# A two-layer kernel on one Trainium2 core: the skewed read of the attention band and the buffers around it

## The reference

```python
x = L0_attn_x                                   # (4, 512, 128) f32
xn = _layernorm(x)
x = x + _L0_attn_ref(xn, ...) + _L0_ffn_ref(xn, ...)      # windowed attention; 16 experts, top 4
xn = _layernorm(x)
return x + _L1_attn_ref(xn, ...) + _L1_ffn_ref(xn, ...)   # full attention; 8 experts, top 2
```

```python
strain = disp_win - disp[:, :, :, None, :]                # (B, nh, T, 64, 16)
logits = gelu(strain @ W_strain + rel_emb @ W_pos) @ W_bond - 10.0 * sigmoid(gelu(strain @ W_dmg + b_dmg) @ W_dmg_out + b)
weights = softmax(where(cmask, logits, -inf), axis=-1)    # over the 64 positions
out = einsum('bntd,bntde->bnte', weights, val_win) @ W_cproj
```

## Time and profile before

| what | value |
|---|---|
| median of 3 runs | 1331.48 us (1328.04 to 1336.38) |
| the profiled execution | 1326.2 us |
| its span | 1324.5 us |
| mean granted TensorE clock | 0.889 of full speed |
| busy | PE 80%, DVE 74%, ACT 62%, POOL 10% |
| first band stage | about 339.6 to 432.3 us of the span |
| second band stage | about 719.0 to 818.3 us |

### The profile page before, as it was taken

How to read it: one execution, slowest core, us unless ns; L and a number is a source line. 1 busy time by engine, 2 the same in 40 slices (tenths; PEclk the granted TensorE clock), 3 DMA queues, 4 the chain that set the end, 5 groups by cost and what they waited for, 6 DMA issues and landing times. The chain is left out here.

```text
span 1324.5 us, 22974 instructions
## 1 busy us (share of the span) xinstructions
PE 1055.4 (80%) x9629; PEld 545.8 (41%) x9629; DVE 981.5 (74%) x1266; ACT 816.5 (62%) x857; POOL 127.7 (10%) x218
## 2 busy tenths in 40 slices
PE   2589999989578599999997468765669989998787
PEld 1233333333466133333333458332235646555332
DVE  6799999999533999999996425349648566666746
ACT  1689999999442699999996512310155564665354
POOL 3000000000100000000001001405400000000630
PEclk9799999999788799999999678775679898999788
DMA  7300000000392200000000860002113432422110
GB/s 259 102 2 1 1 2 1 2 2 1 87 246 52 49 1 1 1 1 2 1 1 0 229 154 21 0 0 82 46 30 99 128 96 81 143 75 62 46 35 24
DMA packets 66886, 71.71 MB, mean 54 GB/s; under 512 B 5892, under 2 KB 58592, under 8 KB 65760
## 3 DMA queue, kind: packets, MB, share of 16 engines
q1 hardware_dynamic: 63456, 49.28, 12.7%
q0 software_dynamic: 3328, 20.98, 6.9%
HBM read 46.12 MB, written 20.97 MB: 51 GB/s over the span
## 5 line engine op out<-in xcount | busy, mean ns | idle before, releaser
L535 DVE SCALAR_TENSOR_TENSOR ring<-AD,PT 128x1808 f32<-128x1808 f32 (+15 forms) x128 | 284.3, 2221 | 3.8 <-POOLq L517 3.2
L680 PE MATMUL LG<-ring,lred 128*32 128x456 f32 (+15 forms) x2048 | 232.2, 573 | 1.3 <-ACT ring L632 1.3
L1598 ACT ACTIVATE EX<-SS 128x1024 f32<-128x1024 f32 x128 | 130.9, 1028 | 105.3 <-PE SS L1469 104.4
L1687 DVE TENSOR_REDUCE MX<-SS 128x2 f32<-128x1024 f32 x128 | 153.0, 1215 | 52.8 <-PE SS L1469 52.3
L622 ACT ACTIVATE ring<-ring 128x3616 f32<-128x3616 f32 (+15 forms) x50 | 169.9, 3399 | 3.7 <-DVE ring L535 3.7
L702 PE MATMUL SD<-DS,eyes 96*32 96x456 bf16 (+15 forms) x2496 | 157.5, 372 | 9.2 <-ACT ring L627 7.2
L630 ACT ACTIVATE ring<-ring 128x1824 f32<-128x1824 f32 (+15 forms) x78 | 141.0, 1808 | 0.0
L702 PEld LDWEIGHTS SD<-DS,eyes 96*32 96x32 bf16 x2496 | 58.1, 96 | 152.9 <-ACT ring L627 57.3
L1469 PE MATMUL SS<-KS,QS 32*128 32x512 f32 x256 | 75.2, 585 | 51.1 <-DVE MX L1687 46.0
L535 DVE SCALAR_TENSOR_TENSOR ring<-AD,bdmg 128x1808 f32<-128x1808 f32 (+15 forms) x50 | 110.7, 2214 | 0.0
L715 PE MATMUL PY<-w2T,xg 128*128 128x128 f32 x512 | 74.2, 288 | 35.2 <-DVE xg L560 35.2
(11 more groups left out here) (300 smaller groups left out, 1486.7 us busy)
## 6 DMA issues: line engine op xcount, KB each, us to landing
wide<-band POOLq DMA_DIRECT2D x16, 1024.0 KB, 11.5
w1s<-in_L_ffn_W SPq DMA_DIRECT2D x39, 256.0 KB, 3.0
w2s<-in_L_ffn_W SPq DMA_DIRECT2D x39, 256.0 KB, 3.0
band<-zs SPq DMA_DIRECT2D x8, 1024.0 KB, 8.3
band<-Z SPq DMA_DIRECT2D x4, 1024.0 KB, 8.7
xs<-Z SPq DMA_DIRECT2D x4, 640.0 KB, 8.7
xl<-xs SPq DMA_DIRECT2D x10, 256.0 KB, 2.9
ys<-yo SPq DMA_DIRECT2D x10, 256.0 KB, 3.0
```

What stands on the lines that cost most here:

```text
L535: return v.scalar_tensor_tensor(out=ring[:, slot, s, :, t0:T], in0=AD[:, s, :, j + t0:j + T], scalar=extra, in1=AD[:, s, :, PAD + t0:PAD + T],
L680: mm = pe.matmul(LG[32 * b:32 * b + 32, par, s, t0:T], lred[:, s, n % 4, :], ring[:, slot, s, b, t0:T], start=(n % 4 == 0), stop=(n % 4 == 3))
L1598: act.activation(EX[:, Q % 2, hh:hh + 2, t, :], SS[:, slot, :, :], ACT.Exp, scale=SCALE1).then_inc(freed[slot], 1)
L1687: v.tensor_reduce(MX[:, t, p // 2, hh:hh + 2], SS[:, slot, :, :], AX.X, ALU.max).then_inc(freed[slot], 1)
```

## The change

Three things in the band stage, and small moves that make room for them.

1. `zd` becomes two tiles, `diffs[0]` and `diffs[1]`, which are the two halves of `wtT` (not needed before turn(0)). DVE now waits, from k = 2 on, for the exponential of k-2, and no longer for that of k-1. In exchange the first copy into `wtT`, on DVE and on ACT, waits for all four exponentials.
2. The reads fetch only what lies in the band: for each block of 16 rows the 16 + 63 = 79 slots that its windows reach, in 8 groups, so 1,264 bytes a piece instead of 16 KB a row. A tile has eight such reads. What they leave out has to be zero, so POOL clears the `wide` tiles at the start of each stage.
3. `wide` has three buffers instead of two (16 KB more on each partition), and the reads are issued by SP and not by POOL: write 0, write 1, read 0, write 2, read 1, write 3, read 2, read 3.

`rtT` moves into `w1T`, `rc` into Z, which are free by then.

```diff
@@ the tiles
-            zd = sb(f"zd{g}", [P, 32, JQ, 4], F32, sm)
-            if g == G - 1:
-                rtT = sb("rtT", [E0, NT, P], F32, sm)
-            wide = sb(f"wide{g}", [P, 2, NG, P, 4], F32, sm)
+            rtT = w1T[0:E0, 0:NT, :]
+            wide = sb(f"wide{g}", [P, WIDE, NG, P, 4], F32, sm)      # WIDE = 3
+            diffs = [wtT[:, 16 * n:16 * n + 16, :].rearrange("p a t -> p (a t)").rearrange("p (n q j) -> p n q j", n=32, j=4) for n in range(2)]
-            rc = sb(f"rc{g}", [P, 2, P], F32, sm)
+            rc = Z[:, 0, 0:2 * P].rearrange("p (a t) -> p a t", a=2)
@@ POOL
+                for n in range(WIDE):
+                    pool.memset(wide[:, n], 0.0).then_inc(wide_zero, 1)
                 pool.memset(vp[:], 0.0).then_inc(vp_zero, 1)
-                def read(k):
-                    pool.wait_ge(d_out[k], 16 * (g + 1))
-                    if k >= 2:
-                        pool.wait_ge(band_pe, 8 * (M0 + k - 1))
-                    for h in range(2):
-                        rows = dram_rows(band, (k * 2 + h) * 64 * 32 * P, [[32 * P - 4, 64], [1, 32 * P]])
-                        pool.dma_start(wide[64 * h:64 * h + 64, k % 2].rearrange("r g s n -> r (g s n)"), rows).then_inc(d_in[k], 16)
-                for k in range(NT):
-                    read(k)
@@ SP                                                            # BLK = 16, SPAN = 79
+                def read(k):
+                    sp.wait_ge(wide_zero, WIDE * g + min(k, WIDE - 1) + 1)
+                    sp.wait_ge(d_out[k], 16 * (g + 1))
+                    if k >= WIDE:
+                        sp.wait_ge(band_pe, 8 * (M0 + k - WIDE + 1))
+                    for i in range(P // BLK):
+                        r0 = BLK * i
+                        s0 = r0 % 64
+                        rows = dram_rows(band, (k * P + r0) * 32 * P + 4 * (s0 - r0 % 64), [[32 * P - 4, BLK], [4 * P, NG], [1, 4 * SPAN]])
+                        sp.dma_start(wide[r0:r0 + BLK, k % WIDE, :, s0:s0 + SPAN, :].rearrange("r g s n -> r g (s n)"), rows
+                                     ).then_inc(d_in[k], 16)
-                for k in range(NT):
+                write(0)
+                for k in range(1, NT):
                     write(k)
+                    read(k - 1)
+                read(NT - 1)
@@ DVE and ACT
-                    if k >= 1:
-                        v.wait_ge(ex_ready, m)
                     ...
+                    if k >= 2:
+                        v.wait_ge(ex_ready, m - 1)
-                    v.tensor_tensor(zd[:], zt, ...
+                    v.tensor_tensor(diffs[par], zt, ...
                 def turn(k):
+                    if k == 0:
+                        v.wait_ge(ex_ready, M0 + NT)          # the same on ACT
```

More of the change, by code:

```diff
@@ L48 @@
 RING = 4
+WIDE = 3
+BLK = 16
+SPAN = BLK + WIN - 1
 PE_ITEMS = (1, 2, 4, 6, 7)
@@ L481, in first_layer @@
         sem(n) for n in ("band_pe", "band_act", "band_dve", "vw_pe", "vw_sb", "nd_pe", "rc_ready", "att_ready"))
-    vp_zero, side_pe, side_sb = sem("vp_zero"), sem("side_pe"), sem("side_sb")
+    vp_zero, wide_zero, side_pe, side_sb = sem("vp_zero"), sem("wide_zero"), sem("side_pe"), sem("side_sb")
     for g in range(G):
@@ L826, in weigh @@
                     v.wait_ge(mx_ready, m + 1)
-                    v.tensor_tensor(zd[:], zt, mx[:, par].unsqueeze(2).unsqueeze(3).to_broadcast([P, 32, JQ, 4]),
+                    if k >= 2:
+                        v.wait_ge(ex_ready, m - 1)
+                    v.tensor_tensor(diffs[par], zt, mx[:, par].unsqueeze(2).unsqueeze(3).to_broadcast([P, 32, JQ, 4]),
                                     ALU.subtract).then_inc(zs_ready, 1)
                 def turn(k):
+                    if k == 0:
+                        v.wait_ge(ex_ready, M0 + NT)
                     for i in range(1, 8, 2):
@@ L837, in divide @@
                     v.wait_ge(nd_pe, m + 1)
-                    v.reciprocal(rc[:], summed(k)[:, 0:2, :]).then_inc(rc_ready, 1)
+                    v.reciprocal(rc, summed(k)[:, 0:2, :]).then_inc(rc_ready, 1)
                     v.wait_ge(rc_ready, m + 1)
-                    v.tensor_tensor(attT[:, g, :, P * ti:P * ti + P], summed(k)[:, 2:4, :], rc[:], ALU.mult).then_inc(att_ready, 1)
+                    v.tensor_tensor(attT[:, g, :, P * ti:P * ti + P], summed(k)[:, 2:4, :], rc, ALU.mult).then_inc(att_ready, 1)
                 def bias(i):
@@ L860, in weigh @@
                         act.wait_ge(d_out[k - 2], 16 * (g + 1))
-                    act.activation(zs[:, k % 2].rearrange("p g s n -> p g n s"), zd[:].rearrange("p (g n) q j -> p g n (q j)", n=4), ACT.Exp
+                    act.activation(zs[:, k % 2].rearrange("p g s n -> p g n s"), diffs[k % 2].rearrange("p (g n) q j -> p g n (q j)", n=4), ACT.Exp
                                    ).then_inc(ex_ready, 1)
@@ L869, in side @@
                         act.wait_ge(side_pe, i + 1)
-                        act.copy(rtT[:], WB[0:E0, 2]).then_inc(side_sb, 1)
+                        act.copy(rtT, WB[0:E0, 2]).then_inc(side_sb, 1)
                 def values(k):
@@ L882, in turn @@
                 def turn(k):
+                    if k == 0:
+                        act.wait_ge(ex_ready, M0 + NT)
                     for i in range(0, 8, 2):
@@ L936, in turn @@
                 def turn(k):
-                    m, par = M0 + k, k % 2
-                    pe.wait_ge(d_in[k], 32 * (g + 1))
+                    m, par = M0 + k, k % WIDE
+                    pe.wait_ge(d_in[k], 16 * (P // BLK) * (g + 1))
                     for i in range(8):
```

## The result

The changed kernel takes 1309.81 us in the median (1307.18 to 1312.09), the kernel before 1332.08 us beside it: a ratio of 0.9834, 95% interval 0.9802 to 0.9867, 22 us less. The profiled execution took 1307.18 us, its span is 1305.5. I had said 1293 with a range of 1279 to 1316: faster, as forecast, but by 22 us and not by 39.

What follows compares the result with a forecast made beforehand. It took the two band stages as losing time in weigh's DVE/ACT alternation and PE's "issue" waits in gathers. Savings of 38.9 us less 4 gave -35: 1291.2 from the profiled 1326.2, 1296.5 from the median; forecast 1293, range 1279 to 1316.

Steps and rivals of the forecast that it cites:

- Part 1: In weigh, two difference tiles allow turn(0) at about 364 instead of 372.2, gaining 8.1 and 1.4 us a stage.
- Part 2, the rate: Band-stage reads: 8.5 us for a tile of 1.29 MB, between 5.0 and 12.3, as blocks in flight overlap imperfectly.
- the half-rate rival: Band-stage 16-partition reads run one after the other at half rate, 12.3 us a tile: 1310.5 us; chance 0.19.
- Part 2, the "issue" waits: In each stage's first two gathers, PE's 21.8 us of waits shrink to 4 us, as smaller pieces delay instruction fetches less.
- the 35 forecast: Both band stages together: 38.9 us saved, less 4 us of remaining "issue" waits, gives -35 us.
- the whole waits: Rival: the gathers' "issue" waits stay whole whatever the size of a piece, saving 17 us: 1309; chance 0.13.
- the prediction's own sign: For the band stages: the sum would be wrong if they shrink by less than 10 us each.
- The 38.9 us: Both band stages' saving, 16.5 and 22.4 us: 17.1 from earlier start and ACT's copies, 21.8 from "issue" waits and clock.
- the 43 us of the lower end: Range's low end, 1279 us: both stages save 18.7 + 24.4 with 5.0 us a tile and all waits gone.
- Part 3: Band-stage buffers and POOL: third buffer frees reads 2 and 3, POOL's memsets hidden, rc and rtT moves 0: cost 0.

Runs made afterwards that it cites:

- e5: The changed kernel with the reads of tiles 1 to 3 cut to one slot, leaving out most data: ratio 0.973 to the kernel before.
- e10: The changed kernel with the reads of before, two of 64 whole 16 KB rows, issued by SP into three wide tiles: ratio 0.9894 to the kernel before.
- e11: The changed kernel with 64-row blocks, in pieces of 2,032 bytes: ratio 0.9907 to the kernel before.
- e9: The changed kernel with 32-row blocks and two wide tiles instead of three: ratio 0.9853 to the kernel before.
- e6: The changed kernel with 32-row blocks and two queues, SP reading rows 0 to 63 and POOL 64 to 127: ratio 0.9731 to the kernel before.
- e7: The changed kernel with 32-row blocks and each write cut into four DMAs: ratio 0.9723 to the kernel before.
- e8: The changed kernel with 32-row blocks issued in the order 0, 2, 1, 3: ratio 0.9739 to the kernel before.

## Why the prediction was right, and why its size was not

*Part 1.* Exponentials at 346.2, 350.7, 355.3 and 360.2 us, where I had 346.3, 350.9, 355.6 and 360.2. Write 1 was just in time or not quite: the fourth exponential waited 1.1 us for it, and in the second stage the third waited 1.8 us for write 0, which cost nothing since read 0 came later still. Right.

*Part 2, the rate.* I took 8.5 us for a tile, between 5.0 and 12.3. Read 0 went at 127 GB/s, 10.2 us for its 1.29 MB; turn(0) began 30.7 and 30.3 us into the stages instead of 27.9. The first mis-sized term: 2.8 + 2.4 = 5 us. What I had against the half-rate rival, that blocks in flight overlap, is the step that failed, for read 0 (127 GB/s) and for read 1 (137, 0.82 MB from 374 to 380). The rival was not right as a whole either: reads 2 and 3 ran at 188 GB/s (1.50 MB from 386 to 394), so blocks do overlap there, and no turn after turn(0) waited for a read.

*Part 2, the "issue" waits.* "Instruction fetch has a sixth to wait", 4 us left of 21.8. They are 9.8 us (3.9, 0.55, 4.8, 0.6), and the lower clock behind them comes on top: gather 0's stretches are 16.9 and 17.1 instead of 12.4 and 12.2, gather 1's 13.9 and 15.3 instead of 11.9 each. Together 14.8 us against the 4 allowed. This was the larger error, and the mechanism behind it was half wrong: traffic causes the waits (e5) by making the fetch late, but the size of its pieces doesn't matter (e10, e11). Gather 1's wait went because the traffic of a stage now ends at 398 us, before that gather's need, and not because the pieces shrank. Gather 0 still meets write 3 and read 2.

These two make 5 + 11 = 16 us, the difference between the 35 forecast and the 19 by which the span shrank.

*The time itself.* That 1309.8 lies within the range says little for the sum. It is 17 us from the forecast, and it is the time of two rivals, 1310.5 for the half rate and 1309 for the whole waits, which had 0.32 together. Each was right in one half: the rate in read 0, the waits in gather 0. By the prediction's own sign the sum was wrong, as the first stage shrank by some 7 us and not by 10.

*Sums that were wrong on record.* The 38.9 us are split wrongly. By the prediction's own stretches the earlier start is 2 x 4.7 us and ACT's copies 2 x 1.4, 12.2 together and not 17.1; that leaves 26.7 us, not 21.8, for the waits and the clock behind them, and 1314 for the rival in which they stay. And the 43 us of the lower end, taken from 1326.2 to 1331.5, give 1283 to 1288 and not 1279.

*Part 3.* I wrote that the third buffer "frees reads 2 and 3" and gave it no price, because no turn would wait for them. e9 prices it with 32-row blocks: 1.1% of the time, about 15 us. No turn but turn(0) waits for a read there either; what it costs is the later end of the traffic, the waits in gather 1 and the clock behind them. POOL's memsets were hidden, as said: done at 350.0, vp at 353.4, the first read issued at 355.4. rc and rtT cost nothing that shows: the first stage's last two gather stretches take 11.7 and 9.5 us, where I had 11.9 and 9.5.

*What stays open.* The traces show the instruction packet late and PE going on behind it; they don't tell what in the queues makes it start late, only that neither the size of a piece, nor the length of a DMA, nor POOL's queue is it. And why the blocks of read 0 share the partitions so little, and those of reads 2 and 3 more, no run tells.

Of the kernels that compute everything, e1, e6, e7 and e8 are the fastest, the same within their intervals, and e1, the change with blocks of 32 rows, is the simplest: 0.974, its interval below that of the change.

## What to carry to other kernels

When a transfer is cut to save bytes, look first at how many partitions each cut one writes: 16 rows at a time moved 38% fewer bytes than 64 whole rows and read 0 took longer than the 64-row reads would (10.2 against 10.0 us at 210 GB/s; with whole rows, e10, turn(0) started 30.2 us into the stage, with the change 30.7), while 32 rows kept the full rate. And in a long unrolled program a wait of PE with no cause that the profile names, beside full DMA queues, is a cost of the traffic: what helps is to have the traffic over before the engine gets to that stretch of the program, so buffers that let transfers run ahead pay there even if no instruction ever waits for the data.

## What the runs showed of the hardware that was not expected

- The rate of a read by the partitions that one DMA writes: 127 GB/s for 16, 210 for 32, 212 for 64; a second queue on the other half of the partitions added a fifth. These are rates of read 0. Blocks further down the queue overlap more: 188 GB/s for 16 partitions, and for 32 with the order changed 296 and 244 (215 and 224 in order).
- PE's waits with the cause "issue" in a long unrolled stretch end 1.2 to 1.7 us after a 16 KB packet of the queue q8, "instruction", and with the data queues full that packet started 4.4 us later than with them empty.
- SP's issue of a DMA slows with the queues: 0.63 us for one in read 0, 1.08 in read 1, up to 1.75, and 1.00 in reads 2 and 3 against 0.53 in e5, where they carry almost nothing (the tile wide of the changed kernel: issues, and landing):

```profile
L812 SPq DMA_DIRECT2D wide<-band x64: 302/604/1753, 355.4 to 761.1; - x64
...
DMA to landing us min/median/max: 4.6/10.9/13.9
```
